# Six of thirteen chunk products of the second sorted part on ScalarE instead of GpSimd, in a graph layer on one core

## The reference

```python
def _L0_gnn_ref(X, edge_row, edge_col, edge_val, W, b):
    msgs = edge_val[:, None] * X[edge_col]
    h = jax.ops.segment_sum(msgs, edge_row, num_segments=N_NODES)
    return h @ W.T + b
...
xn = _layernorm(x, axis=-1)
x = x + _L0_gnn_ref(xn, src, dst, edge_weight, L0_gnn_W, L0_gnn_b) + _L0_mix_ref(xn[None], ...)[0]
x = x + _L0_ffn_ref(_layernorm(x, axis=-1)[None], ...)[0]
```

## Time and profile before

| | us |
|---|---|
| median of 3 runs (lowest, highest) | 1005.84 (1001.59, 1016.77) |
| the profiled execution | 1003.73 |
| its span, from first to last instruction | 1002.0 |
| busy in the span: TensorE, VectorE | 806.0, 674.4 |
| busy in the span: GpSimd, ScalarE | 584.5, 416.7 |

### The profile page before, as it was taken

One profiled execution on the slowest core, in us unless ns is written; L12 is line 12 of the kernel. 1 busy time (PEld: TensorE's weight loads), 2 busy tenths in 40 slices (PEclk: granted clock), 3 DMA queues, 4 the chain that ended last, 5 costly groups with the idle time before them and its releaser, 6 DMA issues.

```text
span 1002.0 us, 14025 instructions
## 1 busy us (share of the span) xinstructions
PE 806.0 (80%) x4353; PEld 651.1 (65%) x4353; DVE 674.4 (67%) x1936; ACT 416.7 (42%) x1008; POOL 584.5 (58%) x648
## 2 busy tenths in 40 slices
PE   7879858888786697788875787778777687999997
PEld 6659747676674364465553565566555564999997
DVE  8889649998864444354454568667657668856676
ACT  3638734585580232223322232223223225766652
POOL 3947686878887665666565556656656600333353
PEclk9989979989999798899897979878879789999999
DMA  7210132322333332323232233323223521000000
GB/s 231 85 48 2 37 93 71 88 83 87 91 88 110 93 85 84 100 79 112 75 103 84 75 94 90 105 78 111 85 86 99 82 46 52 12 17 23 27 27 31
DMA packets 38994, 76.87 MB, mean 77 GB/s; under 512 B 9812, under 2 KB 22537, under 8 KB 38921
## 3 DMA queue, kind: packets, MB, share of 16 engines
q0 software_dynamic: 21120, 57.70, 21.1%
q1 hardware_dynamic: 17800, 18.29, 5.6%
HBM read 69.48 MB, written 6.48 MB: 76 GB/s over the span
## 4 chain that ended last, share of the span: by engine, by line
PE 34%; another core or an unknown queue 16%; DVE 11%; ACT 9%; issue 8%; DVEq 1%; POOLq 0%; POOL 0%; ACTq 0%
PE bank L2000 13%; PE bank L1791 5%; PE bank L1842 5%; DVE X L1281 4%; ACT OIA L816 3%; PE bank L1916 2%; PE bank L1749 2%; PE bank L1628 1%; DVE ARENA L1269 1%; PE bank L1849 1%; PE bank L1919 1%; PE bank L1857 1%; PE bank L1918 1%; DVE ST L1021 1%
## 5 line engine op out<-in xcount | busy, mean ns | idle before, releaser
L699 POOL DMA_INDIRECT ARENA<-xg_rows,ARENA x440 | 426.6, 969 | 236.4 <-issue 119.4
L1281 DVE TENSOR_TENSOR X<-bank,X 128x256 f32 x440 | 185.0, 420 | 243.0 <-PE bank L1791 113.5
L1791 PE MATMUL bank<-ARENA 128*128 128x256 f32 x880 | 238.9, 411 | 58.8 <-DVE X L1281 48.4
L1791 PEld LDWEIGHTS bank<-ARENA 128*128 128x128 f32 x880 | 170.4, 204 | 106.8 <-DVE X L1281 56.2
L1269 DVE TENSOR_SCALAR ARENA<-iota,ARENA 128x128 f32<-128x128 f32 x440 | 153.8, 355 | 0.0
L1749 PE MATMUL bank<-OIA,ASA 128*128 128x128 f32 x676 | 94.1, 306 | 15.9 <-DVE ASA L1199 5.8
L1749 PEld LDWEIGHTS bank<-OIA,ASA 128*128 128x128 f32 x676 | 92.8, 222 | 19.6 <-issue 18.5
L816 ACT ACTIVATE OIA<-iota,LANE 128x128 f32<-128x128 f32 x286 | 85.9, 388 | 13.9 <-PE bank L1749 13.6
L1842 PE MATMUL bank<-QKVW,XT 128*128 128x512 f32 x100 | 55.2, 703 | 14.6 <-ACT XT L853 14.6
L984 ACT ACTIVATE HF<-bank,FB 128x262 f32<-128x262 f32 (+1 forms) x96 | 46.9, 488 | 40.8 <-DVE HFL L1566 20.5
L1916 PE MATMUL bank<-W,HS 128*128 128x256 f32 x100 | 36.9, 503 | 29.2 <-ACT HS L908 27.4
(11 more groups left out here) (317 smaller groups left out, 1586.8 us busy)
## 6 DMA issues: line engine op xcount, KB each, us to landing
ARENA<-xg_rows,ARENA POOLq DMA_INDIRECT x440
FW1A<-in_exp_w SPq DMA_DIRECT2D x8, 512.0 KB
xg_rows<-XGS SPq DMA_DIRECT2D x12, 256.0 KB, 2.1
out<-YO SPq DMA_DIRECT2D x24, 128.0 KB, 1.7
X<-in_x SPq DMA_DIRECT2D x1, 1664.0 KB, 12.4
X<-in_x SPq DMA_DIRECT2D x1, 1536.0 KB, 8.0
FW<-in_exp_w SPq DMA_DIRECT2D x2, 512.0 KB, 4.4
QKVW<-in_qkv_wT SPq DMA_DIRECT2D x1, 768.0 KB
```

The source lines that it names most:

```text
L699: pool.indirect_dma_start(RING[:, at, :], None, xg_dram, bass.IndirectOffsetOnAxis(ap=SIX[:, c:c + 1], axis=0)).then_inc(gathered[at // HA ...
L1281: V.tensor_tensor(xt, pair_bank(pair)[:, half * C:(half + 1) * C], xt, ALU.add).then_inc(x_added, 1)
L1791: ins = T.matmul(pair_bank(pair)[:, u * C:(u + 1) * C], SEL[:, t % 2 * HAND + k, :], RING[:, h * HAND + k, :], start=True, stop=True)
```

## The change

For groups 13 to 31 ScalarE makes the products of the first six chunks (BY_ACT) of ASA's right half, one instruction of 128x64 for each chunk, with EPC's column as scale and a column of zeros as bias. GpSimd makes the other seven in one instruction. ScalarE does so between the copies of group G - 2 and the lanes of group G, and waits for `lh_ready` of G and for `grp_done` of G - 2 ahead of it. A new semaphore, `cp_ready`, tells TensorE (before group G) and VectorE (before it overwrites LHA) that they are done.

```diff
+        BY_ACT = 6
+
+        def shared(G):
+
+            return G > GA
...
                 lh, into = buffer_of(LHA, LHB, G), buffer_of(ASA, ASB, G)
-                made = pool.tensor_tensor(into[:, :, LC:2 * LC], lh, per_chunk(EPC, G, LC), ALU.mult)
+                lo = BY_ACT if shared(G) else 0
+                made = pool.tensor_tensor(into[:, lo:GC, LC:2 * LC], lh[:, lo:GC, :], per_chunk(EPC, G, LC)[:, lo:GC, :], ALU.mult)
...
+            def edge_columns(G):
+                act.wait_ge(lh_ready, G + 1)
+                act.wait_ge(grp_done, before(G) + 1)
+                lh, into = buffer_of(LHA, LHB, G), buffer_of(ASA, ASB, G)
+                for k in range(BY_ACT):
+                    ins = act.activation(into[:, k, LC:2 * LC], lh[:, k, :], ACT.Identity, bias=zeros[:, 0:1],
+                                         scale=EPC[:, G * GC + k:G * GC + k + 1])
+                ins.then_inc(cp_ready, 1)
...
                 if n >= 2:
                     evacuate(G - 2)
+                if shared(G):
+                    edge_columns(G)
                 lanes(G)
...
                     dve.wait_ge(ap_ready, of + 1)
+                    if shared(of):
+                        dve.wait_ge(cp_ready, of - GA)
...
                 pe.wait_ge(ap_ready, G + 1)
+                if shared(G):
+                    pe.wait_ge(cp_ready, G - GA)
```

More of the change, by code:

```diff
@@ L316, in gps_layer_program @@
         ap_ready = sem("ap_ready")
+        cp_ready = sem("cp_ready")
         oi_ready = [sem(f"oi_ready{s}") for s in range(4)]
```

## The result

The changed kernel takes 1039.97 us (median of 4 runs, 1027.52 to 1043.62) where the kernel before takes 1008.48 (1001.59 to 1016.77): a ratio of 1.0382, 95% interval 1.0303 to 1.0461. The ratio is taken over the fast runs alone; the quotient of the two medians is 1.031. The changed kernel is slower, and its time lies above 1032, the upper end of my range. The profiled span grew from 1002.0 to 1038.8 us, 36.8 us.

A forecast was written before the change was run, and what follows sets the result against it. GpSimd's 9.10 us round was taken as the bound. Group 30 starts at 172.1 + 7 x 18.8 + 3 x 1.0 = 306.7, 11.5 us late; 1003.73 + 11.5 = 1015.2, forecast as 1016 us, range 1000 to 1032.

The forecast's parts named there:

- The amounts: Groups 13 to 31: six ScalarE products in 2.1 us, GpSimd's product at 1.10 us, its round about 8.6 us.
- GpSimd as the clock of the part: Second sorted part: GpSimd has next to no pause and sets the pace, 9.10 us a round.
- a shorter product gives some of that back: VectorE's OJ row waits for GpSimd's product; a shorter one releases it sooner, at most 0.5 us a loop, 0.3 taken.
- The start: TensorE's first affected groups: group 15 3.7 us late, group 16 at 172.1 instead of 169.61.
- The loop: OIA, TensorE's group, VectorE's LHA two groups on, ScalarE's products and lanes: 18.8 us a turn, seven turns.
- the five small instructions: VectorE work ahead of LHA in three of the seven loops from group 16 to 30: 1.0 us each.
- rival (2): TensorE's clock falls more often while waiting for ScalarE: 1028 us, or 1033 if in every loop; chance 0.2.
- 7 to 18: Whole kernel: us slower than before through ScalarE's wait for LHA ahead of the lanes; chance 0.6.
- (1): GpSimd's pace carries over: 17 rounds shorten by 0.5 to 0.73 us each, 994 us; chance 0.12.
- (3): The wait is hidden because TensorE is late for other reasons; gain and loss cancel, 1004 us; chance 0.08.
- D: Later reading, from the experiments: GpSimd's 1.1 us pause between gather runs is too short for TensorE's results to come through.
- E: Later reading, from the experiments: GpSimd's round gets shorter than the loop, so it waits for LHA and shifts its next gathers.

The follow-up runs named there:

- f3: Kernel before, plus a useless GpSimd product of 0.65 us in each of groups 13 to 31: 1.0124 on the second kind of chip.
- h4: Kernel before with six of the thirteen chunks of GpSimd's product left out in groups 13 to 31: 885.03 us, 0.9909 on the second kind of chip.
- g2: Kernel before with six of the thirteen chunks of GpSimd's product left out in groups 13 to 31: 1031.68 us, 1.0219 on the first kind of chip.
- e4: Kernel before with six of the thirteen chunks of GpSimd's product left out, in an earlier run on the first kind of chip: 1033.35 us, 1.024.
- g3: Kernel before with six of GpSimd's thirteen chunks left out and a useless 0.65 us GpSimd product added: 1004.60 us, 0.9867 on the first kind of chip.
- g1: The changed kernel itself, run again on the first kind of chip, against the kernel before: 1.0322.
- g4: Changed kernel plus a useless GpSimd product of 0.65 us in groups 13 to 31: 1.0183 against the kernel before, first kind of chip.

## Why the prediction was wrong, step by step

- **The amounts held.** Six products in 2.10 us (2.1 forecast), 428 ns each (434); the product of GpSimd 0.95 us (1.10 taken, between the ends 0.86 and 1.10); its own round 8.4 us (8.6). VectorE's OJ row still ends just behind GpSimd's product where the two meet, and takes less for it (1.25 us from 195.82 and 1.62 us from 218.23, against 2.37).
- **GpSimd as the clock of the part held on one kind of chip.** f3 (0.0124 x 896 = 11.1 us for 17 x 0.65) and h4 (-8.5 us) show it there. On the kind that I forecast for it was wrong in sign: the step "Over 19 products that is 9.5 us, at most 13.9. It counts only if nothing else takes the place of GpSimd" bounds the worth of the lighter product by nothing on one side and 13.9 us of gain on the other. It has to be bounded below nothing too: g2 and e4 measured a loss of 23 us, and g3 shows that the shorter time on GpSimd is its cause. This is the step that failed, and it stands in the sum as "a shorter product gives some of that back, at most 0.5, and I take 0.3": a gain of 0.3 us in each turn, or none at worst. On the first kind putting the time back takes a turn from 21.8 and 21.0 us (changed kernel, g1; group 16 to 30) to 19.9 (g4), so the shorter product cost 1 to 2 us a turn, and g4's longest stretches from OIA to LHA are then 12.8 us, the same as on the second kind. The trace had the hint: the kernel before had VectorE waits with "remote" as releaser, and ScalarE's copy of group 17 came 3.3 us behind the end of its row. I had read the OJ row's release by the product as the only coupling between GpSimd's round and the others.
- **The start** was mis-sized both ways: group 15 came 1.8 us late (3.7), group 16 4.4 us (2.5).
- **The loop** was the right mechanism for the order of ScalarE, and its size was off: 19.2 us a turn forecast (18.8 and three sevenths of 1.0), 19.9 measured on the second kind, 21.8 and 21.0 on the first. The term that was off is the stretch from the end of OIA to the end of LHA two groups on, taken as 11.3 from samples in which the group took 3.1 to 3.6 us, less 0.3 for the release. It is 12.8 on the second kind from group 17 to 23 and 11.8 and 11.5 in the next two, with a group of 4.8 to 5.6 us. On the first kind the seven stretches from group 16 on take 12.9 to 15.2 us, 14.1 in the mean: the group takes 4.8 to 5.9 us, three of them have the five small instructions in them (some 0.9), and in the turn shown VectorE's first add comes 0.9 us behind the end of the pair's rows. In the terms of the sum, the start is 1.9 us off (173.98 against 172.1) and the seven turns 17.8 (152.4 against 134.6). That every start behind OIA is at the low clock was my rival (2) "in every one", 1033: its condition came true on both kinds. Its price of 2.5 us a turn was too high for the second kind, where the stretch is at most 1.5 us over the 11.3, and the 27 to 32 us of the first kind take the worth of the lighter GpSimd besides. On the second kind the whole comes to 17.3 us (911.19 against 893.93), inside the 7 to 18 that I gave the mechanism, though with the low clock in every turn, which those 7 to 18 left out; on the first it is 27 to 32.
- **The other rivals.** (1), that GpSimd's lighter round carries over, is true of the second kind when nothing else is changed (0.991), and of no run with ScalarE's products ahead of the lanes. (3), gain and loss cancelling, is nearest to lanes first with the time put back (1.005), not to the change.
- **What is shown and what isn't.** Shown on the first kind: the lighter GpSimd alone loses 23 us, its time put back takes 27 us off the lighter kernel and 11 us off the changed one; the wait alone and the load alone cost some 5 us each in the part and little or nothing that the kernel's time tells; lanes first still leaves 1.027. Shown by the semaphore's times: TensorE's results are late on the first kind and not on the second, and with the lighter product some of them miss the pause between two runs of gathers. The parts don't quite add up (lighter 1.022, changed with the time put back 1.018, changed 1.032); that both lengthen the same loop is my reading. Nor need the lighter product do the same harm in both kernels: of the 14 groups from 17 to 30, 9 have their result recorded as at most 0.02 us late in the changed kernel (4 have no record), against 3 in g2_light. Not shown: how the late results turn into 23 us (D, E or both), by what way the shorter product costs the changed kernel its 11 us, and what makes the results late.
- No version was found that beats the kernel before. The lighter one that is 0.9% faster on the second kind leaves work out; with the work on ScalarE behind the lanes and GpSimd slowed it is 0.5% slower there, and the same without the slowing was not tried there.

## What to carry to other kernels

Bound the worth of a lighter engine below nothing as well, and test that half of a change alone, however harmless it looks: here the half meant as the gain was by itself a loss of 23 us on one kind of chip. Where idle time is ended by "remote", or by an engine whose row was over long before, measure from the start of the producing row to the start of the consuming one, since rows alone give too short a loop. An instruction that waits doesn't belong in front of one that could have run ahead, even on an engine with time to spare (1.021 against 1.005).

## What the runs showed of the hardware

- Chips differ by more than the change. The kernel before takes 1008 to 1010 us in three comparisons and 893.5 to 896.2 in three others; the profiled runs have granted clocks of 0.89 to 0.91 in the first and 0.95 to 0.96 in the others, and the sign of one edit differs between the kinds (1.022 and 0.991). Most of the difference lies where GpSimd only gathers: 486 to 507 us against 392 to 398.
- On the first kind the results of TensorE reach ScalarE 3.5 us and VectorE 2.5 and 5.9 us after the end of its rows while GpSimd issues gathers (g2_light, group 20 and the pairs behind it); most of them come 1.2 to 1.4 us behind the end of a run's last gather (kernel before), or 3.4 us behind it when the next run begins after 1.12 us (g2_light, e4_light_pool). On the second kind the same group of the same code passes on its result within 0.02 us. The rows don't show what holds them up, and no run here settles it.
- TensorE's group of 26 matmuls takes 3.06 us with a granted clock of 1.00 (2.4 GHz; changed kernel, 205.4 to 208.4). Behind the pauses of 3 to 4.2 us for OIA it takes 4.6 to 5.9 in the changed kernel, on both kinds of chip: group 18, behind 3.90 us without work, takes 4.77 with a granted clock of 0.64 (195.5 to 200.2), group 28, behind 3.30 us, takes 5.88 with 0.50, the lower level of 1.2 GHz (306.0 to 311.7).
